# Three attention sums over 50,000 edges: the next block's exponential moved between ACT's second and last third, its score chain ahead of the sums

## The reference

```
def _segment_softmax(alpha, dst, n):
    amax = segment_max(alpha, dst)
    ex = exp(alpha - amax[dst])
    den = segment_sum(ex, dst)
    return ex / (den[dst] + 1e-16)

def _rgat(x, src, dst, etype, W, Q, K, b, heads, out_ch, n):
    xw = einsum('ni,rio->rno', x, W)          # two relations
    out_i = xw[etype, dst]
    out_j = xw[etype, src]
    alpha = leaky_relu(out_i @ Q + out_j @ K, 0.2)
    alpha = _segment_softmax(alpha, dst, n)
    msg = (out_j.reshape(-1, heads, out_ch) * alpha[..., None]).reshape(-1, heads * out_ch)
    return segment_sum(msg, dst, n) + b

h = relu(_rgat(h, ..., W1, q1, k1, b1, 4, 128, n))         # attention 1: 4 heads of 128
h = h + relu(_rgat(h, ..., W2, q2, k2, b2, 4, 128, n))     # attention 2: 4 heads of 128
h = relu(_rgat(h, ..., W3, q3, k3, b3, 1, 128, n))         # attention 3: 1 head of 128
```

## Time and profile before

| | value |
|---|---|
| median of three runs | 6739.39 us |
| the profiled execution | 6756.12 us, span 6754.3 us |
| busy over the span | PE 66%, DVE 48%, ACT 30%, POOL 53% |
| mean granted TensorE clock | 0.769 of full speed |
| L1198 gathers on POOL | 1296 instructions, 1599.8 us busy, mean 1234 ns |
| L1295 sums on PE | 4320 records, 1241.6 us busy, mean 452 ns |
| L1231 scaling on ACT | 3312 instructions, 985.1 us busy, mean 398 ns |
| ACT's idle time before L1231 | 492.5 us, of which 446.7 until the weights (L1423) |

### The profile page before, as it was taken

One profiled execution on the slowest core, in us unless ns is written; L12 is line 12 of the kernel. 1 busy time (PEld: TensorE's weight loads), 2 busy tenths in 40 slices (PEclk: granted clock), 3 DMA queues, 4 the chain that ended last, 5 costly groups with the idle time before them and its releaser, 6 DMA issues. The chain is left out here.

```text
span 6754.3 us, 80950 instructions
## 1 busy us (share of the span) xinstructions
PE 4441.0 (66%) x17924; PEld 3187.3 (47%) x17925; DVE 3214.4 (48%) x7726; ACT 2012.5 (30%) x4713; POOL 3593.5 (53%) x2941
## 2 busy tenths in 40 slices
PE   5699620885766778577677444467777777765553
PEld 5588610543555554455557333344545555443332
DVE  6566556213544522444443233343777777523334
ACT  0122200002655511455550122212555555410000
POOL 0244310467766647776647778721444444228885
PEclk9999855887887889787776555556999999876555
DMA  0000012225655523665532222222222222223333
GB/s 7 24 11 11 8 33 65 68 65 126 170 149 140 140 66 73 157 162 146 145 100 53 44 45 46 45 60 59 58 58 59 58 58 58 59 79 84 84 84 73
DMA packets 487821, 511.66 MB, mean 76 GB/s; under 512 B 307562, under 2 KB 372575, under 8 KB 487289
## 3 DMA queue, kind: packets, MB, share of 16 engines
q0 software_dynamic: 359872, 381.65, 23.6%
q1 hardware_dynamic: 127670, 127.35, 6.8%
HBM read 440.64 MB, written 65.22 MB: 75 GB/s over the span
## 5 line engine op out<-in xcount | busy, mean ns | idle before, releaser
L1198 POOL DMA_INDIRECT sum_gx_sb<-scratch_xw,keep_k_row_step_sb x1296 | 1599.8, 1234 | 564.1 <-issue 361.9
L1295 PE MATMUL sum_a_ps<-sum_gx_sb,sum_sel_sb 125*125 125x258 f32 (+1 forms) x4320 | 1241.6, 452 | 557.7 <-ACT sum_gx_sb L1231 234.9
L1295 PEld LDWEIGHTS sum_a_ps<-sum_gx_sb,sum_sel_sb 125*125 125x125 f32 x4320 | 955.9, 247 | 757.8 <-issue 563.2
L1231 ACT ACTIVATE sum_gx_sb<-sum_gx_sb,sum_wt_sb 125x129 f32<-125x129 f32 x3312 | 985.1, 398 | 492.5 <-DVE sum_wt_sb L1423 446.7
L2354 POOL DMA_INDIRECT filter_gx_sb<-scratch_h,keep_k_src_step_sb x432 | 520.6, 1205 | 678.0 <-DVEq L2495 531.7
L2782 POOL DMA_INDIRECT source_gx_sb<-scratch_h,source_grouped_sb x432 | 537.0, 1243 | 156.0 <-issue 118.9
L2794 PE MATMUL source_s_ps<-source_gx_sb,source_sel_sb 125*125 125x257 f32 x864 | 378.9, 615 | 313.6 <-DMA source_gx_sb<-scratch_h,source_grouped_sb 311.5
L1107 POOL DMA_INDIRECT scratch_grouped<-keep_k_value_sb,keep_k_place_sb x400 | 477.9, 1195 | 123.5 <-issue 123.5
L2400 PE MATMUL filter_ps<-filter_m_sb,filter_h_sb 128*125 128x256 f32 x1760 | 439.5, 406 | 39.9 <-DVE filter_f_sb L2464 39.9
L2794 PEld LDWEIGHTS source_s_ps<-source_gx_sb,source_sel_sb 125*125 125x125 f32 x864 | 252.5, 306 | 440.0 <-issue 196.3
L2400 PEld LDWEIGHTS filter_ps<-filter_m_sb,filter_h_sb 128*125 128x125 f32 x1760 | 343.9, 201 | 186.0 <-issue 132.7
(11 more groups left out here) (504 smaller groups left out, 7082.6 us busy)
## 6 DMA issues: line engine op xcount, KB each, us to landing
sum_gx_sb<-scratch_xw,keep_k_row_step_sb POOLq DMA_INDIRECT x1296
scratch_xw<-gate_xsb_sb SPq DMA_DIRECT2D x50, 253.9 KB
scratch_xw<-attend_xsb_sb SPq DMA_DIRECT2D x50, 253.9 KB
filter_ea_sb<-in_ea_t SPq DMA_DIRECT2D x444, 24.4 KB
filter_gx_sb<-scratch_h,keep_k_src_step_sb POOLq DMA_INDIRECT x432
source_gx_sb<-scratch_h,source_grouped_sb POOLq DMA_INDIRECT x432
sum_mk_sb<-scratch_masks SPq DMA_DIRECT2D x72, 93.9 KB
scratch_grouped<-keep_k_value_sb,keep_k_place_sb POOLq DMA_INDIRECT x400
```

Of the source, the lines that this page charges most:

```text
L1198: nc.gpsimd.indirect_dma_start(out=gx[:, q, j, :], out_offset=None, in_=table, in_offset=bass.IndirectOffsetOnAxis(ap=keep["row_step"][:, ...
L1231: last = nc.scalar.activation(here, here, ACT.Copy, scale=wt[q][:, h, j:j + 1])
L1295: last = mm(psa[b][0:P, half, 0:BF], sel[:, 0, p, j, :], gx[:, q, at, half * BF:(half + 1) * BF], **flags)
```

## The change

ACT: the exponential of block s+1 stands before the last third of the scaling of block s, no longer behind it. TensorE: `list_ends` and `turn_carry` for block s+1 stand before the first third of the sums of block s (before: behind the first and behind the second), and `turn_weights` stands behind the second third (before: behind the last). DVE: `spread_over_tiles`, the last pick and `shift` stand before the add of the first third, `grow` behind it; `take_weights` and then `score` for s+2 stand between the adds of the second and of the last third; the pick of the next first third stays behind the add of the last.

```diff
--- before.py
+++ after.py
@@ -1223,9 +1223,11 @@
                 act.wait_ge(ready, s + 1)
                 nc.scalar.activation(wexp[:], dw[:], ACT.Exp).then_inc(exped, 1)
 
-            def scale(s, q):
+            def scale(s, q, ahead):
                 act.wait_ge(weights_made, s + 1)
                 for j in range(T):
+                    if j == T - HF and ahead:
+                        weights(s + 1)
                     for h in range(H - 1 if j < shared * HF else H):
                         here = gx[:, q, j, h * (W + 1):(h + 1) * (W + 1)]
                         last = nc.scalar.activation(here, here, ACT.Copy, scale=wt[q][:, h, j:j + 1])
@@ -1240,12 +1242,9 @@
             weights(0)
             with act.Fori(0, NS // 3 - 1) as i:
                 for q in range(3):
-                    scale(3 * i + q, q)
-                    weights(3 * i + q + 1)
+                    scale(3 * i + q, q, True)
             for q in range(3):
-                scale(NS - 3 + q, q)
-                if q < 2:
-                    weights(NS - 2 + q)
+                scale(NS - 3 + q, q, q < 2)
 
         @block.tensor
         def _(pe):
@@ -1317,19 +1316,17 @@
 
             def block_of(s, q, ahead):
                 spans = part_tiles(nc, keep, s, slice(1, 2), mybir.EngineType.PE)
+                if ahead:
+                    list_ends(s + 1)
+                    turn_carry(s + 1)
                 for p in range(PARTS):
                     pe.wait_ge(parted, s * PARTS + p + 1)
                     with pe.If(spans[p] < 1):
                         sums(s, q, p, True)
                     with pe.If(spans[p] > 0):
                         sums(s, q, p, False)
-                    if ahead:
-                        if p == 0:
-                            list_ends(s + 1)
-                        elif p == 1:
-                            turn_carry(s + 1)
-                        else:
-                            turn_weights(s + 1, (q + 1) % 3)
+                    if ahead and p == 1:
+                        turn_weights(s + 1, (q + 1) % 3)
                 if ahead > 1:
                     turn_scores(s + 2)
 
@@ -1475,20 +1472,21 @@
                 if ahead:
                     spread_in_tiles(s + 1, nxt, i + (q + 1) // 3 + 1)
                 pick(s, q, 1)
-                add_part(s, 0, firsts, spans)
                 if ahead:
                     spread_over_tiles(s + 1)
                 pick(s, q, 2)
+                if ahead:
+                    shift(s + 1, nxt)
+                add_part(s, 0, firsts, spans)
+                if ahead:
+                    grow(s + 1)
                 add_part(s, 1, firsts, spans)
                 if ahead:
-                    shift(s + 1, nxt)
+                    take_weights(s + 1, nxt)
                 if ahead > 1:
                     score(s + 2, later, i + (q + 2) // 3 + 1)
-                if ahead:
-                    grow(s + 1)
                 add_part(s, 2, firsts, spans)
                 if ahead:
-                    take_weights(s + 1, nxt)
                     pick(s + 1, nxt, 0)
 
             score(0, 0, 1)
```

## The result

The changed kernel took 7083.93 us, median of four runs (7065.57 to 7099.76), against 6740.18 us (6736.36 to 6741.33): a ratio of 1.051, 95% interval 1.0484 to 1.0536. The forecast was 7150 us, range 7010 to 7300. Direction, mechanism and range held; the size was 66 us too large.

The account below looks back on a forecast made before the run. Gathers bound easy blocks at 18.1 us; the change makes the DVE and TensorE loop 10.5 + 14.7 = 25.2 us. Attentions add +201 +192 +20 = +413 us to the 6739.4 median: about 7150 us, range 7010 to 7300.

Parts of the forecast that it names:

- The bound: Wide attentions: plain blocks follow POOL's gathers at 18.1 us; after the change DVE and TensorE's loop takes 25.2 us.
- The gap: TensorE, from the end of a last third to the next first third: 10.5 us, where 3.7 stood.
- The links: Serial steps in TensorE's gap (add, pick, loads, scan, second pick, spread, carry): 6.00 + 2.48 + 0.44 + 1.04 + 0.58 us.
- E: The moment a last third of TensorE's sums ends; times to the next first third count from it.
- TensorE's own work: TensorE's three thirds plus matmuls for the next weights in a plain wide block: 14.7 us, first third 6.2.
- Borders and loop edges: Extra time at tile borders, 40 us, and at five DVE loop edges, 24 us, per wide attention.
- Worth nothing: ACT's earlier exponential gains nothing: scaling done at E+19.4, TensorE wants it at E+21.4, a cover of 2.0 us.
- A: Rival: all blocks fall to POOL's pace, needing a gap of at most 3.4 us; 6544 us, chance 0.05.
- D: Rival: the change does nothing, since gathers set the pace before and after; 6740 us, chance 0.02.
- B: Rival: DVE's table loads hide in its wait for the last add, saving 3.57 us per block; 6910 us, chance 0.09.
- C: Rival: TensorE's clock stays low beyond the first third, adding 4 us per block; 7420 us, chance 0.04.
- The clock: TensorE's first third after idling runs slowly: put at 6.2 us, not 3.72; the skill's rule gives some 170 us less.

Follow-up runs that it names:

- the chain alone: Kernel before, with TensorE's listing of ends and carry turn ahead of the first third and DVE's spread over tiles ahead of the first add: 7143.52 us, ratio 1.0603.

## Why the prediction was right, and where its size was off

**The bound.** It said that gathers set the pace of plain blocks at 18.1 us and that the change makes the loop of DVE and TensorE the bound. In the changed kernel the sixteen plain periods of the first attention are 22.8 to 24.7 us, and POOL's waits rose to 251.4 and 252.7 us, where "about 240 us or more" was named. Right.

**The gap.** 10.5 forecast, 10.56 measured in one block and 10.5 on the mean. The links agree too: the scan starts at E + 6.09 for 6.00 (1962.25), and the spread over tiles ends at E + 9.93 for 9.96 (1965.84 + 0.25). The two runs that take one link out confirm it: 3.0 us of gap and 189 us for the loads, 129 us for the carry's turn (with the shift moved along) against the run with ACT's order of before (7079.18 - 6949.97), and 298 us for both (7079.18 - 6781.33), the last two across occasions.

**TensorE's own work** is the mis-sized term. It was put at 6.2 + 0.1 + 3.72 + 0.9 + 3.75 = 14.7 us. The first two thirds together took 9.59 instead of 10.0:

```profile
1966.72:1972.90 6.18, 6.18 (x18) 4.94 (x19) 1.20 (x6) 4.56 (x16) 0.03 (x1) 0.61 0.28 92
1972.90:1976.20 3.30, 3.30 (x16) 2.60 (x14) 1.34 (x5) 0.43 (x2) 2.47 (x3) 1.00 0.12 17
```

These are the stretches up to 1972.9 and behind it, with a granted clock of 0.61, then 1.00; the engine had idled before the first. And the matmuls for the next weights took 0.35 instead of 0.9 (1976.31 to 1976.66): the 0.9 was read in the old order, where DVE made the growth factor only at 1953.05 and its matmul followed at 1953.19, while now that factor is made at 1974.93, before the matmuls are reached. A last third without a border takes 3.75 (1952.41), so a plain block does its work in 9.59 + 0.35 + 3.75 = 13.7 us (13.5 on the mean of plain blocks). With the gap it is 24.3 here, 24.0 on that mean, and 23.9 by the sixteen periods of the first attention below 24.8. That is 1.2 to 1.3 us less than 25.2, on 68 blocks 82 to 88 us. The sums of the stages agree: 159.7 for +201, 153.7 for +192, 9.8 for +20, in all 323 for 413, 90 us less. Against the medians the miss looks smaller, 66 us, because the stages are those of one execution each, the one after 18 us below its median and the one before 16 us above.

**Borders and loop edges** were put at 64 us per attention. The 35 periods of the first attention come to 899.8 us, the first of them to 19.5; the other 34 are 68 us above 34 plain ones. Right in sum, and in part by luck, since the gaps split it otherwise than 40 and 24. The loop has four edges in an attention, not five: the gaps there are 13.28, 14.04, 13.67 and 15.18 us, together 14 us above four of 10.5. That leaves some 54 us for borders, where 40 was put.

**The exponential.** "Worth nothing" held (7079.18 with it put back, 7083.93 with it), with a cover of 3.3 us for the 2.0 forecast. The exponential started at E + 12.2 (1968.34), two microseconds sooner than the 14.3 taken from the old order. What I had not seen is how much that rests on DVE's new order: on the kernel before, the same ACT order costs 324 us.

**The rivals.** A needed a gap of 3.4 us and D a loop near 18; both fell with the gap. B (loads hidden) was priced at 6910, 240 us under the forecast; the changed kernel does not hide them. With the loads really taken out of the gap the run gave 6895, close to 6910 by luck: it won 189 us from a time that was itself 66 lower. C (low clock into the second third) did not occur: 1.00 from 1972.9 on, and the second third ends 3.5 us behind the first in every one of the twenty plain blocks. Its price was mis-added besides: a whole second third at half speed would cost 3.7 us more, not 2.8.

**The clock.** The forecast left aside the advice of the Trainium skill, "TensorE: Matmul & The Clock Gate", section "What's actually happening", which puts the slow start at under 1% of a typical kernel's span. The run with unread matmuls in the gap bears the forecast out: 1.8 to 2.0 us per plain block, which over 68 blocks would be 122 to 136 us or 1.7 to 1.9% of the span. That is an estimate; the run as a whole won only 46 to 57 us, since the added matmuls cost something elsewhere. By that rule the forecast would have been about 6980, a hundred below the measurement; the rows came within 66.

## What to carry to other kernels

When engines with hand-written orders form a loop, lay the loop out as one serial line from the end of one matmul group to the start of the next, with register loads and issue gaps as links of their own, and compare its length with the pace of the other engines before moving anything: a step started earlier on its producer helps only if its consumer's queue isn't blocked on it. Most of what a block gained or lost here stood between two groups of sums; the rest was TensorE's clock behind such a wait. Test the parts of a change each alone, and each with the others in place: here the chain alone cost 403 us and the exponential alone 324, while the whole cost 344, and with the rest in place the exponential cost nothing that the spread of the runs lets one see (7083.93 against 7079.18). A third part, DVE's earlier shift and weights, made the difference. So the sum of single tests doesn't tell the price. The chain was never taken out with that third part left in, so its price there is not known.

## What the runs showed of the hardware that was not expected

- Loads of six table values into DVE's registers hold DVE up in each block: in the wide attentions it idles 2.7 to 3.8 us before the scan (3.50 in the one shown), over a tenth of a plain period, and 0.2 to 0.3 where the loads stand elsewhere. At the loop's edges it is 5.8 to 7.5 us, and 3.3 to 4.8 without the loads. Only their place decides whether anybody waits: in the gap they cost 189 us over the kernel, behind the second pick of the kernel before they are 19 us cheaper than before the scan.
- Matmuls that only keep TensorE busy do raise the granted clock (0.93 against 0.76 over the stretch 1640 to 2500), but run slowly themselves when they start behind a wait: the same 48 records took 5.62, 7.48 and 8.55 us in three blocks, at granted clocks of 1.00, 0.74 and 0.64. The 0.17 of clock over that stretch went with 22.6 us less in the first wide attention (899.8 to 877.2 between the first and last weights) and 24.2 in the second.
